# A decoder layer's out-projection as three single-pass products of halves, with all five engines' lists drawn up anew

## The chip, the cores and the metric

One core of one Trainium2 chip runs the whole kernel. The metric is the device time of one execution in microseconds (us). Five engines work side by side, each through its own list of instructions: TensorE (PE in the profile, its weight loads PEld), VectorE (DVE), ScalarE (ACT), GpSimd (POOL) and SyncE (SP, which here only issues transfers). They wait for each other by semaphores.

## The reference, cut to what matters

A post-norm decoder layer over 64 independent sequences (x is 64 x 256 x 256, the context 64 x 120 x 256). Only the first of its three parts is touched by the arithmetic of the change:

```python
zxbcdt = u @ W_in.T                      # u: 256 tokens x 256; z 512, xBC 544, dt 8 columns
xBC = silu(causal_conv4(xBC) + conv_b);  dt = softplus(dt + dt_bias)
y, _ = ssd(x * dt[..., None], A * dt, Bm, Cm, 64)      # 8 heads of 64
y = (y + x * D[:, None]).reshape(b, L, 512) * silu(z)
y = y * rsqrt(mean(y * y, axis=-1) + 1e-05) * norm_w
x = layernorm(x + y @ W_out.T)           # W_out: 256 x 512: the out-projection
x = layernorm(x + cross_attention(ctx, x))   # 8 heads, 120 + 256 keys
x = layernorm(x + twisted_ffn(x))            # three coupling cycles of a small net
```

## The kernel before

Every sequence is a set of steps (functions with the sequence's number as argument), and each engine has a written-out list of calls. After a fill for the first two sequences, a loop `for p in range(2, NSEQ - 1)` (61 passes) works on four sequences at a time: the last cycles of the feed-forward of f-2 and f-1, the attention of `f = p - 2`, the mixer of `a = p - 1`, and the first projections of `m = p`. After the loop a drain finishes the last ones. The order inside each engine's list is fixed text; nothing is reordered at run time, so an instruction whose semaphore is late holds all that stands behind it on its engine.

The steps that matter here, with their lines in the profile:

- PE: `project`/`product3` (L263) is a product of fp32 numbers as three passes of halves (hi x hi, lo x hi, hi x lo), used for w_in, wq, wkv and cw1. `y_pair(a, q)` (L338) multiplies the scan matrix Lm by xdt; `mean_square(a)` (L361) sums the squares; `out_proj(a)` (L350) is the out-projection in plain fp32: per sequence eight products of 128x128 by 128x256, which the profile records as sixteen matmuls. `scores(f, i, j)` (L443) are three products of halves of an attention score tile, `turn` (L455) transposes probabilities, `k_tile(a, 0)` (L263, kv_hi by wkv_hi) makes the first keys of sequence a, `layer(f-1, ., .)` (L518) is the feed-forward.
- DVE: `y_out(a, q)` (L1628) adds D*x to y straight from PSUM; `x_low` (L1487) and `kv_low(a, 1)` (L1719) subtract the high half from a value to get the low half; `x1_sum` (L1647), `x1_stats`, `x1_mean` (L1661), `x1_norm` (L1671) are the first layernorm, whose reciprocal root POOL makes (`mix`, L2504 to L2507); `pre(f-1, 0)` (L1852) updates the feed-forward's input; `weights(0, 3)` (L1903) scales w_out by norm_w at set-up.
- POOL: `gated(a, q)` (L2481) is g = yD * silu(z); `squares` (L2487, L2489) adds the squares that ACT made (`square`, L955).
- ACT: `x_high(m)` (L881) casts a 128x512 tile to the high half.

`out_proj(a)` waits for POOL's last `gated` (`l_g`), and comes right behind `mean_square(a)` in PE's list. `k_tile(a, 0)` waits for `kv_low(a, 1)`'s semaphore.

## Time and profile before

| | |
|---|---|
| median of 3 runs | 3686.18 us (3681.73 to 3687.39) |
| profiled execution, its own time | 3687.81 us |
| its span (first to last record) | 3685.6 us |
| mean granted TensorE clock | 0.991 |
| PE busy | 3613.6 us (98%) |
| DVE busy | 3246.4 us (88%) |
| ACT busy | 3072.9 us (83%) |
| POOL busy | 1788.0 us (49%) |

Busy times are unions of records, so an engine whose instructions follow each other with small gaps shows less than 100% though it never waits for anyone. 2.2 us of the execution's time lie outside its span. The execution profiled is 1.6 us above the median.

### The profile page before, as it was taken

How to read it: one execution, taken by the hardware profiler on the slowest of the kernel's cores; microseconds unless marked ns; L12 is line 12 of the kernel's file. 1: busy time of each engine (PE TensorE's matmuls, PEld its weight loads, DVE VectorE, ACT ScalarE, POOL GpSimd, SP SyncE). 2: the span in 40 equal slices, each digit the busy share in tenths (PEclk: the TensorE clock that was granted, in tenths of full speed). 3: DMA queues.
4: the chain of work that ended last, by engine and by line, in shares of the span. 5: the costliest groups of instructions: out<-in, count | busy, mean ns of one | idle time of the engine just before them, and what ended most of it. 6: DMA issues, size and time to landing. Idle time of an engine off the chain costs nothing.

```text
span 3685.6 us, 79670 instructions
## 1 busy us (share of the span) xinstructions
PE 3613.6 (98%) x26752; PEld 3085.0 (84%) x26752; DVE 3246.4 (88%) x7970; ACT 3072.9 (83%) x7559; POOL 1788.0 (49%) x3084
## 2 busy tenths in 40 slices
PE   5999999999999999999999999999999999999997
PEld 4888888888888888888888888888888888888885
DVE  7888988988988989889889889889898898898884
ACT  5788888888888888888888888888888888888884
POOL 4355454454554554554544545545545545445442
PEclk8999999999999999999999999999999999999998
DMA  3212212112122122122121121221221221211210
GB/s 100 59 37 67 59 42 67 52 49 67 39 63 64 37 67 64 37 67 58 43 67 53 48 67 39 63 65 37 67 64 37 67 60 42 67 55 46 67 34 21
DMA packets 312358, 203.28 MB, mean 55 GB/s; under 512 B 55056, under 2 KB 310928, under 8 KB 311952
## 3 DMA queue, kind: packets, MB, share of 16 engines
q1 hardware_dynamic: 311952, 198.20, 18.7%
q8 instruction: 215, 3.52, 0.4%
q14 instruction: 191, 1.56, 0.1%
HBM read 180.17 MB, written 17.96 MB: 54 GB/s over the span
## 4 chain that ended last, share of the span: by engine, by line
PE 93%; DVE 3%; ACT 1%; issue 1%; SPq 1%; DMA 1%; POOL 1%; POOLq 0%; DVEq 0%; ACTq 0%
PE psum L263 35%; PE psum L455 10%; PE psum L471 9%; PE psum L443 8%; PE psum L350 6%; PE psum L482 6%; PE psum L518 5%; PE psum L338 5%; PE psum L524 2%; PE psum L533 2%; PE psum L322 1%; PE psum L495 1%; PE psum L383 1%; PE psum L361 1%; PE psum L545 1%
## 5 line engine op out<-in xcount | busy, mean ns | idle before, releaser
L1015 ACT ACTIVATE prob<-psum,nmax 128x376 f32<-128x376 f32 x1024 | 588.7, 582 | 36.0 <-DVE nmax L1741 35.0
L2471 POOL TENSOR_TENSOR Lm<-Lm,G 128x384 f32<-128x384 f32 x512 | 497.3, 1011 | 81.8 <-DVE out_sb L1869 68.8
L1741 DVE TENSOR_REDUCE nmax<-psum 128x2 f32<-128x752 f32 x512 | 472.8, 934 | 44.2 <-PE psum L443 39.4
L455 PE MATMUL psum<-ident,prob 128*128 128x128 f32 (+1 forms) x3072 | 486.4, 278 | 3.1 <-DVE probT L1764 1.7
L455 PEld LDWEIGHTS psum<-ident,prob 128*128 128x128 f32 (+1 forms) x3072 | 354.8, 141 | 87.0 <-issue 46.5
L1493 DVE SCALAR_TENSOR_TENSOR u<-psum,par,u 128x255 f32<-128x255 f32 (+5 forms) x960 | 408.2, 467 | 12.0 <-ACT u L914 1.5
L2458 POOL TENSOR_SCALAR_AFFINE_SELECT Lm<-Lm 128x256 f32<-128x256 f32 x512 | 193.0, 416 | 375.7 <-DMA Lm<-cum_row 375.5
L2526 POOL TENSOR_TENSOR h_a<-h_a,cpl 128x512 f32<-128x512 f32 x64 | 83.0, 1297 | 594.0 <-DVE h_pre L1852 594.0
L471 PE MATMUL psum<-probT,V 128*64 128x256 f32 (+1 forms) x3072 | 360.5, 383 | 0.4 <-ACT probT L1025 0.4
L263 PE MATMUL psum<-x_hi,w_in_hi 128*128 128x256 f32 (+1 forms) x1152 | 344.8, 299 | 13.0 <-DVE w_in_lo L1897 7.6
L263 PE MATMUL psum<-x_hi,w_in_lo 128*128 128x256 f32 (+1 forms) x1152 | 325.4, 282 | 0.0
L263 PE MATMUL psum<-x_lo,w_in_hi 128*128 128x256 f32 (+1 forms) x1152 | 324.7, 282 | 0.0
L1025 ACT ACTIVATE probT<-psum 128x384 f32<-128x384 f32 x512 | 254.7, 498 | 79.6 <-PE psum L455 72.2
L1764 DVE COPY probT<-psum 128x384 f32<-128x384 f32 x512 | 281.4, 550 | 30.4 <-PE psum L455 30.2
L471 PEld LDWEIGHTS psum<-probT,V 128*64 128x64 f32 (+1 forms) x3072 | 208.6, 136 | 110.9 <-ACT probT L1025 0.4
L948 ACT ACTIVATE Lm<-Lm,ncum 128x256 f32<-128x256 f32 x512 | 264.8, 517 | 2.6 <-DVE ncum L1605 1.9
L263 PEld LDWEIGHTS psum<-x_hi,w_in_hi 128*128 128x128 f32 (+1 forms) x1152 | 214.0, 186 | 29.6 <-issue 21.2
L350 PE MATMUL psum<-w_out_sb,g 128*128 128x256 f32 x1024 | 236.8, 384 | 1.3 <-DVE dt_a L1507 1.3
L482 PE MATMUL psum<-wo_sb,oT 128*128 128x256 f32 x1024 | 235.5, 381 | 1.7 <-DVE probT L1764 1.4
L518 PE MATMUL psum<-h,cw_sb 128*128 128x256 f32 x768 | 209.3, 395 | 10.2 <-ACT h L1058 8.4
L1015 ACT ACTIVATION_READ_ACCUMULATOR prob<-psum,nmax 128x1 f32 x1024 | 218.7, 214 | 0.0
L2481 POOL TENSOR_TENSOR g<-xc,gate 128x256 f32<-128x256 f32 x256 | 206.5, 826 | 19.5 <-DVE xc L1628 19.4
(227 smaller groups left out, 11668.6 us busy)
## 6 DMA issues: line engine op xcount, KB each, us to landing
Lm<-cum_row SPq DMA_DIRECT2D x64, 1024.0 KB, 5.2
Lm<-cum_row SPq DMA_DIRECT2D x64, 512.0 KB, 6.6
invT<-inv_row SPq DMA_DIRECT2D x256, 128.0 KB, 3.0
xT_sb<-in_xT SPq DMA_DIRECT2D x64, 256.0 KB, 2.7
x_sb<-in_x SPq DMA_DIRECT2D x64, 256.0 KB, 5.8
result<-out_sb SPq DMA_DIRECT2D x64, 256.0 KB, 2.4
inv_row<-inv_t SPq DMA_DIRECT2D x512, 1.0 KB
ctx_sb<-in_ctx SPq DMA_DIRECT2D x64, 120.0 KB, 6.4
```

Source lines behind the costliest of these rows:

```text
L263: t = mm(dst, a, b, start=n == 1, stop=n == 3 * KT)
L350: t = mm(banks[b][:, i * D:(i + 1) * D], g[:, c, i * P:(i + 1) * P], w_out_sb[:, c, :], start=c == 0, stop=c == CT - 1)
L443: t = mm(banks[at[k]][:, 0:NK], q_[r, c, i * P:(i + 1) * P], k_[r, c, :], start=m == 0, stop=m == 2)
L455: t = tr(banks[b][0:m, j * P:(j + 1) * P], prob[:, r, j0:j0 + m], ident[:, :])
L471: t = mm(banks[b][k * HD:(k + 1) * HD, at:at + L], V[0:m, j, h * HD:(h + 1) * HD], probT[0:m, (8 * s + h) % HP, j, :], start=j == 0, stop= ...
L482: t = mm(banks[b][:, 0:D], oT[:, c, i * P:(i + 1) * P], wo_sb[:, c, :], start=c == 0, stop=c == CT - 1)
L518: t = mm(b[:, 0:L], cw2_sb[:, k, :], h1[:, k, :], start=k == 0, stop=k == KT - 1)
L1015: act(prob[:, r, :], b[:, 0:NK], ACT.Exp, bias=nmax[:, n:n + 1], accum_out=psum_row[:, n:n + 1]).then_inc(a_exp, 1)
L1493: stt(u[0:rows, c, d:L], src[:, 0:L - d], prm("conv_w", 4 * c + 3 - d, slice(0, rows)), u[0:rows, c, d:L], ALU.mult, ALU.add).then_inc(don ...
L1741: e.tensor_reduce(nmax[:, 2 * n:2 * n + 2], psum[:, b:b + 2, 0:NK], AX.X, ALU.max, negate=True).then_inc(d_max, 1)
L1764: cp(probT[:, (8 * s + 2 * c + k) % HP, :, i * P:(i + 1) * P], b[:, 0:len(JT) * P].rearrange("p (j t) -> p j t", j=len(JT))).then_inc(d_tn, 1)
L2471: t = tt(Lm[:, h, :], Lm[:, h, :], G[:, :], ALU.mult)
```

## The change

The out-projection is computed from halves: g is split into g_hi (ACT, `g_high`) and g_lo (DVE, `g_low`), w_out into w_out_hi and w_out_lo at set-up, and `project4` multiplies hi by hi, hi by lo and lo by hi, 24 products of 128x128 by 128x256 for a sequence. g_lo shares its memory with g, w_out_lo with w_out_sb. The scratch memory that the program keeps for dynamic DMA descriptors is set to 1024. And the lists of all five engines are written in a new order (some 1,500 of the 1,872 lines of the diff; the lines below show its core and one piece of the new order of PE and DVE).

```diff
-        w_out_sb, wo_sb = sb("w_out_sb", [P, CT, D]), sb("wo_sb", [P, CT, D])
+        w_out_hi, (w_out_lo, w_out_sb) = sb("w_out_hi", [P, CT, D], F32R), shared("w_out_lo", "w_out_sb", [P, CT, D])
-        g = sb("g", [P, CT, L])
+        g_hi, (g_lo, g) = sb("g_hi", [P, CT, L], F32R), shared("g_lo", "g", [P, CT, L])
...
+            def project4(dst, hi, lo, w_hi, w_lo, i):
+                tok = slice(i * P, (i + 1) * P)
+                for c in range(CT):
+                    mm(dst, hi[:, c, tok], w_hi[:, c, :], start=c == 0, stop=False)
+                    mm(dst, hi[:, c, tok], w_lo[:, c, :], start=False, stop=False)
+                    t = mm(dst, lo[:, c, tok], w_hi[:, c, :], start=False, stop=c == CT - 1)
+                return t
...
-                pe.wait_ge(l_g, 4 * s + 4)
+                pe.wait_ge(d_gl, 2 * s + 2)
                 for i in range(TT):
-                    for c in range(CT):
-                        t = mm(banks[b][:, i * D:(i + 1) * D], g[:, c, i * P:(i + 1) * P], w_out_sb[:, c, :],
-                               start=c == 0, stop=c == CT - 1)
+                    t = project4(banks[b][:, i * D:(i + 1) * D], g_hi, g_lo, w_out_hi, w_out_lo, i)
...
+            def g_high(s, j):
+                if not live(s):
+                    return
+                sc.wait_ge(l_g, 4 * s + 2 * j + 2)
+                act(g_hi[:, 2 * j:2 * j + 2, :], g[:, 2 * j:2 * j + 2, :], ACT.Copy).then_inc(a_gh, 1)
...
+            def g_low(s, j):
+                if not live(s):
+                    return
+                ve.wait_ge(a_gh, 2 * s + j + 1)
+                ve.wait_ge(a_sq, 4 * s + 2 * j + 2)
+                r = slice(2 * j, 2 * j + 2)
+                tt(g_lo[:, r, :], g[:, r, :], g_hi[:, r, :].bitcast(F32), ALU.subtract).then_inc(d_gl, 1)
...
-                    t.then_inc(set_w, 1)
+                    t.then_inc(set_split, 1)
+                    ve.wait_ge(set_split, 2)
+                    cp(w_out_hi[:, :, :], w_out_sb).then_inc(set_split, 1)
+                    ve.wait_ge(set_split, 3)
+                    tt(w_out_lo[:, :, :], w_out_sb, w_out_hi[:, :, :].bitcast(F32), ALU.subtract).then_inc(set_w, 1)
...
-    nc = bacc.Bacc("TRN2", target_bir_lowering=False, num_devices=1)
+    nc = bacc.Bacc("TRN2", target_bir_lowering=False, num_devices=1, dynamic_dma_scratch_size=1024)
```

PE, in the loop, where the scan's product stands among the attention's scores. Before, `y_pair(a, 0..3)` follows the last product of `q_pair(f, 1)`; it is these rows, and one score tile (`scores(f, 2, 0)`) stands behind it:

```order
L338 MATMUL psum<-Lm,xdt 64x256 x2
L338 MATMUL psum<-Lm,xdt 64x128 x2
L338 MATMUL psum<-Lm,xdt 64x256 x2
L338 MATMUL psum<-Lm,xdt 64x128 x2
L338 MATMUL psum<-Lm,xdt 64x256 x2
L338 MATMUL psum<-Lm,xdt 64x128 x2
L338 MATMUL psum<-Lm,xdt 64x256 x2
L338 MATMUL psum<-Lm,xdt 64x128 x2
L443 MATMUL psum<-k_hi,q_hi 128x376 x2
L443 MATMUL psum<-k_hi,q_lo 128x376 x2
L443 MATMUL psum<-k_lo,q_hi 128x376 x2
L263 MATMUL psum<-x_hi,w_in_hi 80x256
```

In the changed kernel (whose line numbers are 8 to 10 higher):

```order
L451 MATMUL psum<-k_lo,q_hi 128x376 x2
L348 MATMUL psum<-Lm,xdt 64x256 x2
L348 MATMUL psum<-Lm,xdt 64x128 x2
L348 MATMUL psum<-Lm,xdt 64x256 x2
L348 MATMUL psum<-Lm,xdt 64x128 x2
L348 MATMUL psum<-Lm,xdt 64x256 x2
L348 MATMUL psum<-Lm,xdt 64x128 x2
L348 MATMUL psum<-Lm,xdt 64x256 x2
L348 MATMUL psum<-Lm,xdt 64x128 x2
L451 MATMUL psum<-k_hi,q_hi 128x376 x2
L451 MATMUL psum<-k_hi,q_lo 128x376 x2
L451 MATMUL psum<-k_lo,q_hi 128x376 x2
```

One score tile moved ahead of the scan's product, and another one that stood next to a third tile later in the list now stands alone behind it.

DVE, in the loop, from the first `y_out(a, 0)`. Before, between the `y_out`s and the convolution's taps (L1493):

```order
L1628 SCALAR_TENSOR_TENSOR xc<-xc,par,psum 128x256
L1493 SCALAR_TENSOR_TENSOR u<-psum,par,u 80x255
L1507 TENSOR_SCALAR dt_a<-psum,par 8x256
L1493 SCALAR_TENSOR_TENSOR u<-psum,par,u 80x254
L1479 TENSOR_SCALAR x<-x,mv_att,rs_att 128x256
L1733 TENSOR_TENSOR k_lo<-psum,k_hi 128x376
```

In the changed kernel, where `g_low(a, 0)` is L1803 (the second one, `g_low(a, 1)`, comes behind the taps, ahead of `softplus(m)` and `mean_square(a)`):

```order
L1515 SCALAR_TENSOR_TENSOR u<-psum,par,u 80x255
L1529 TENSOR_SCALAR dt_a<-psum,par 8x256
L1515 SCALAR_TENSOR_TENSOR u<-psum,par,u 80x254
L1803 TENSOR_TENSOR g_lo<-g,g_hi 128x512
L1515 SCALAR_TENSOR_TENSOR u<-psum,par,u 80x253
L1515 SCALAR_TENSOR_TENSOR u<-psum,par,u 128x255
```

A 128x512 subtraction entered the stretch that begins with the `y_out`s. At the end of that stretch stands `kv_low(a, 1)`. Before:

```order
L1608 COPY dt_tok<-dc 32x16 x4
L1712 CAST kv_hi<-kv 128x2x256
L1755 STREAM_TRANSPOSE inv_t<-row_inv 128x32
L1719 TENSOR_TENSOR kv_lo<-kv,kv_hi 128x2x256
L1852 TENSOR_TENSOR h_pre<-h_pre,h_a 128x512
```

In the changed kernel:

```order
L1741 TENSOR_TENSOR kv_lo<-kv,kv_hi 128x2x120
L1871 TENSOR_TENSOR h_pre<-h_b,cpl 128x512
L1734 CAST kv_hi<-kv 128x2x256
L1882 TENSOR_TENSOR h_pre<-h_pre,h_a 128x512
L1741 TENSOR_TENSOR kv_lo<-kv,kv_hi 128x2x256
```

`pre(f-1, 0)` (h_pre<-h_pre,h_a) stood behind `kv_low(a, 1)` and stands ahead of it now. Between the first `y_out(a, 0)` and `kv_low(a, 1)` in all, one `top` (a maximum over scores, L1741 before), `bc_silu` (two instructions, L1523 and L1524 before), `x1_keep(a, 0)` (L1680 before), `out_x(f-2, 0)` (L1860 before) left the stretch; two `g_low`, `x_silu(m, 0)` (128x512), `pre(f-1, 0)`, one `out_norm` and one `out_stats` (128x256 each) entered it. In the changed kernel `x1_norm(a, 0)` comes 6 steps behind `x1_mean(a, 1)`, with `kv_high(a, 0)`, `turn_out(f, 6)`, `inverse(f, 0)`, `out_mean(f-2, 0)` and `turn_dc(m)` between.

## Rows read from the trace of the kernel before

**Rows 1.** The page: span, busy time (share of the span), instructions of each engine

```profile
span 3685.6 us, 79670 instructions
PE 3613.6 (98%) x26752; PEld 3085.0 (84%) x26752; DVE 3246.4 (88%) x7970; ACT 3072.9 (83%) x7559; POOL 1788.0 (49%) x3084
```

**Rows 2.** Busy time by stretch: length, engines, granted clock, DMA share, GB/s

```profile
1000.00:2000.00 1000.00, 999.31 (x7470) 854.70 (x7470) 898.54 (x2209) 853.63 (x2107) 498.69 (x859) 1.00 0.19 56
```

**Rows 3.** Timeline of PE around the out-projection: start us, length us, instruction

```profile
1720.14 3.70 PE L350 MATMUL psum<-w_out_sb,g 128*128 128x256 f32 x16
1723.49 0.47 PE L263 MATMUL psum<-x2T_hi,cw_hi 128*128 128x256 f32 x1
1723.79 0.28 PE L263 MATMUL psum<-x2T_hi,cw_lo 128*128 128x256 f32 x1
1723.91 0.28 PE L263 MATMUL psum<-x2T_lo,cw_hi 128*128 128x256 f32 x1
```

**Rows 4.** Timeline of PE from one scan product to the next

```profile
1708.75 2.87 PE L338 MATMUL psum<-Lm,xdt 128*64 128x256 f32 x32
...
1737.98 0.44 PE L263 MATMUL psum<-kv_hi,wkv_hi 128*128 128x376 f32 x1
...
1738.95 0.33 PE L263 MATMUL psum<-kv_lo,wkv_hi 128*128 128x376 f32 x1
1739.30 1.10 PE L518 MATMUL psum<-h,cw_sb 128*128 128x256 f32 x4
...
1764.75 2.82 PE L338 MATMUL psum<-Lm,xdt 128*64 128x256 f32 x32
1767.50 0.44 PE L443 MATMUL psum<-k_hi,q_hi 64*128 64x376 f32 x2
...
1768.20 0.35 PE L263 MATMUL psum<-x_hi,w_in_hi 128*80 128x256 f32 x1
```

**Rows 5.** Timeline of DVE in that pass, with idle before and releaser

```profile
1710.36 0.45 DVE L1628 SCALAR_TENSOR_TENSOR xc<-xc,par,psum 128x256 f32<-128x256 f32 x1
1710.73 0.69 DVE L1487 TENSOR_TENSOR x_lo<-xT_sb,x_hi 128x512 fp32r<-128x512 f32 x1
...
1726.58 0.18 DVE L1661 BATCH_NORM_AGGREGATE mv_mix<-st_mix 128x2 f32<-128x6 f32 x1
...
1729.73 0.41 DVE L1671 TENSOR_SCALAR x_n<-x,mv_mix,rs_mix 128x256 f32<-128x256 f32 x1
...
1733.47 0.41 DVE L1830 TENSOR_SCALAR cpl<-cpl,tf_gain,c_cyc 128x256 f32<-128x256 f32 x1 [0.28 <-ACT cpl L1070]
...
1736.93 0.68 DVE L1719 TENSOR_TENSOR kv_lo<-kv,kv_hi 128x512 fp32r<-128x512 f32 x1
1737.53 0.68 DVE L1852 TENSOR_TENSOR h_pre<-h_pre,h_a 128x512 f32<-128x512 f32 x1
```

**Rows 6.** Timeline of POOL in that pass

```profile
1710.89 2.50 POOL L2481 TENSOR_TENSOR g<-xc,gate 128x256 f32<-128x256 f32 x3 [0.20 <-DVE xc L1628]
...
1714.33 0.75 POOL L2481 TENSOR_TENSOR g<-xc,gate 128x256 f32<-128x256 f32 x1
...
1717.07 1.28 POOL L2487 TENSOR_TENSOR gate<-gate 128x512 f32<-128x512 f32 x1 [0.72 <-ACT gate L955]
...
1727.93 1.03 POOL L2507 TENSOR_TENSOR rs_mix<-ve_mix,minus_half 128x4 f32<-128x4 f32 x1
```

**Rows 7.** ACT in 1000 to 2000 us, groups: count, busy us, mean ns

```profile
L881 ACT ACTIVATE x_hi<-xT_sb 128x512 fp32r<-128x512 f32 x18 | 11.2, 623 | 0.0
```

**Rows 8.** All 64 of DVE's x_low: duration ns, min/median/max

```profile
L1487 DVE TENSOR_TENSOR x_lo<-xT_sb,x_hi x64: 681/684/694, 4.7 to 3500.8; 128x512 fp32r<-128x512 f32 x64
```

**Rows 9.** Timeline of DVE at the start

```profile
13.15 2.03 DVE L1493 SCALAR_TENSOR_TENSOR u<-psum,par,u 128x255 f32<-128x255 f32 x5 [1.09 <-ACT u L914]
18.50 2.84 DVE L1903 TENSOR_SCALAR w_out_sb<-w_out_sb,par 128x256 f32<-128x256 f32 x4 [3.31 <-DMA gw_sb<-in_gw]
```

More of the change, by code:

```diff
@@ L812, in _ @@
             scores(last, 2, 0)
+            turn(last, 3)
+            k_tile(last, 3)
+            scores(last, 2, 1)
+            x2_turn(last - 1)
             v_tile(last, 1)
[L814 to L817 removed]
             turn(last, 4)
@@ L2141, in _ @@
-                k_low(a, 2)
-            last = NSEQ - 1
-            x_dt(last - 1, 1)
+            last = NSEQ - 1
+            top(last - 3, 7)
+            turn_out(last - 3, 10)
+            gain(last - 4, 0)
+            turn_inverse(last - 3, 0)
+            kv_low(last - 2, 0)
+            twisted_part(last - 4, 0)
+            kv_high(last - 2, 1)
+            kv_low(last - 2, 1)
+            pre(last - 4, 0)
+            conv_tap(last - 1, 3, 0)
+            conv_tap(last - 1, 2, 0)
+            inverse(last - 3, 1)
@@ new lines, in _ @@
+            conv_tap(last - 1, 2, 1)
+            context_stats(last - 1)
+            conv_tap(last - 1, 3, 1)
+            conv_tap(last - 1, 3, 2)
+            conv_tap(last - 1, 2, 2)
+            k_low(last - 2, 0)
+            by_token(last - 1)
+            x_silu(last - 1, 1)
+            turn_inverse(last - 3, 1)
+            q_low(last - 2, 0)
+            k_low(last - 2, 1)
+            gain(last - 4, 1)
+            twisted_part(last - 4, 1)
+            x_dt(last - 1, 0)
+            pre(last - 4, 1)
@@ L2149, in _ @@
             bc_low(last - 1)
-            divide(last - 3, 1)
-            top(last - 2, 1)
             out_x(last - 4, 1)
+            turn_out(last - 2, 0)
             out_tw(last - 4, 1, 0)
             out_tw(last - 4, 1, 1)
+            x2_raw(last - 3, 0)
+            x2_stats(last - 3, 0)
+            out_stats(last - 4, 1)
+            out_mean(last - 4, 1)
+            x2_mean(last - 3, 0)
+            out_x(last - 4, 0)
             top(last - 2, 2)
-            turn_out(last - 2, 0)
@@ L2157, in _ @@
-            x2_raw(last - 3, 0)
             gate_silu(last - 1, 1)
-            context_stats(last - 1)
-            out_stats(last - 4, 1)
-            x_low(last)
             q_low(last - 2, 1)
-            out_mean(last - 4, 1)
+            x1_keep(last - 2, 0)
             x2_raw(last - 3, 1)
             x2_stats(last - 3, 1)
+            x2_mean(last - 3, 1)
             top(last - 2, 3)
-            x2_stats(last - 3, 0)
-            context_mean(last - 1)
-            x2_mean(last - 3, 1)
+            top(last - 2, 4)
@@ L2208, in _ @@
-            cum_da(last)
-            x1_mean(last - 1, 1)
-            kv_high(last - 1, 0)
-            turn_out(last - 2, 8)
+            conv_tap(last, 1, 1)
+            conv_tap(last, 0, 1)
+            conv_tap(last, 1, 2)
+            conv_tap(last, 0, 2)
+            g_low(last - 1, 1)
+            x2_high(last - 3)
+            softplus(last)
+            x1_keep(last - 2, 1)
+            mean_square(last - 1)
+            x2_low(last - 3)
+            context_n(last - 1)
+            turn_out(last - 2, 4)
@@ L2212, in _ @@
+            x1_sum(last - 1, 0)
+            x1_sum(last - 1, 1)
+            cum_dt(last)
+            x1_stats(last - 1, 0)
+            x_silu(last, 0)
+            cum_da(last)
+            inverse(last - 2, 0)
+            x1_stats(last - 1, 1)
+            x1_mean(last - 1, 0)
+            cum_scan(last)
+            x1_mean(last - 1, 1)
+            out_norm(last - 4, 1)
+            turn_out(last - 2, 6)
+            turn_inverse(last - 2, 0)
+            top(last - 2, 6)
             x1_norm(last - 1, 0)
-            x1_norm(last - 1, 1)
@@ L2322, in _ @@
             pre(last - 2, 0)
+            k_low(last, 0)
+            divide(last - 1, 0)
             inverse(last - 1, 1)
-            k_low(last, 0)
-            turn_inverse(last - 1, 1)
+            out_stats(last - 3, 0)
+            out_mean(last - 3, 0)
             q_low(last, 0)
+            x1_keep(last, 1)
+            out_norm(last - 3, 0)
             k_low(last, 1)
@@ L2388, in _ @@
             divide(last, 1)
-            out_stats(last - 2, 1)
-            out_mean(last - 2, 1)
             x2_raw(last, 0)
             x2_stats(last, 0)
+            out_x(last - 1, 1)
             x2_mean(last, 0)
-            out_mean(last - 2, 0)
             x2_raw(last, 1)
@@ L2419, in _ @@
             pre(last, 1)
-            out_stats(last - 1, 0)
-            out_mean(last - 1, 0)
-            out_norm(last - 1, 0)
             out_x(last, 1)
@@ L2579, in _ @@
             po.wait_ge(set_dve, 1)
-            weights(0)
+            context(0)
             masked(0, 0)
@@ L2592, in _ @@
             gated(0, 3)
-            context(0)
             squares(0)
+            weights(0)
             inv_rms(0)
```

951 lines of the change are left out of this document (467 added, 484 removed).

## The prediction

> **What bounds the kernel now.** I read the page first: PE is busy 98% of the span, no other engine above 88% [rows 1]. A share over the whole span can hide stages, so the second view is the busy time by stretch: between 1000 and 2000 us PE is busy 999.31 of 1000.00 us at a granted clock of 1.00, DVE 898.54 and ACT 853.63 [rows 2]. The loop is PE's work end to end, and a microsecond taken from PE's list counts as long as nobody else becomes late. Third, the timeline gives the length of a pass: the scan product L338 starts at 1708.75 and again at 1764.75, so a pass takes 56.00 us, and 61 passes are 3416 of the 3685.6 us [rows 1, 4].
>
> The important question is how much room the other engines have, and for DVE the 90% misleads: instructions follow each other there at start-to-start distances below their lengths (L1719 lasts 0.68 and the next starts after 0.60 [rows 5]), and small instructions leave gaps in which nobody is waited for. So I measure a stretch from PE's event that releases DVE to DVE's event that releases PE. `y_out(a, 0)` waits for PE's second scan pair and starts at 1710.36, 1.61 us behind 1708.75 (in the five passes that follow it is 1.61 or 1.62 too). Behind it DVE works down its list to `kv_low(a, 1)`, which ends at 1736.93 + 0.68 = 1737.61, 27.25 us later [rows 5]. `k_tile(a, 0)` needs that and starts at 1737.98 [rows 4]: DVE has 0.37 us of room there. That is less than what the change moves on either engine, and the forecast hangs on it.
>
> **The change part by part, for one pass.**
>
> *The product.* L350 starts at 1720.14; the product behind it starts at 1723.49, and the one behind that at 1723.79: 3.65 us [rows 3]. Single-pass products of 256 columns follow each other at 0.12 (1723.79 to 1723.91 [rows 3]). 24 of them, an entry of 0.08 as the first of such a run has over the others, and one 0.12 to the same point make 24 x 0.12 + 0.08 + 0.12 = 3.08: **-0.57** on PE. By the Trainium skill, page "TensorE: Matmul & The Clock Gate", section "Back-to-back issue gap", products at full clock are N/2.4 + 2.5 ns apart, 109 ns for 256 columns. By that the 24 would take 0.2 us less than by the row, some 13 us in all; the row is of this kernel, with its weight loads, and I keep the row.
>
> *PE's new order.* One score tile, `scores(f, 2, 0)`, moves from the part behind L338 to the part ahead of it. Inside a run three pairs of 376 columns cost 3 x 0.17 = 0.51 (five such products take 1738.95 - 1737.98 = 0.97, the first of them 0.28 [rows 4]). A tile that stands alone costs 1768.20 - 1767.50 = 0.70 [rows 4]; the new list has one more that stands alone, `scores(f, 1, 0)`: 0.19, and 0.07 on the product ahead of it. `layer(f-1, 1, 1)` starts 1739.30 - 1738.95 = 0.35 behind the product ahead of it where 0.17 is the distance [rows 4]; that is a short wait for `h`, which comes from `pre(f-1, 0)`. Since `pre` stands ahead of `kv_low(a, 1)` now, I take 0.19 off. PE's own pass is then 56.00 - 0.57 + 0.26 - 0.19 - 0.05 (one joint fewer between kinds of product) = 55.45.
>
> From L338 to `k_tile(a, 0)` it was 1737.98 - 1708.75 = 29.23 [rows 4] and becomes 29.23 - 0.57 - 0.51 - 0.05 = 28.10. From there to the next L338 it was 26.77 and becomes 26.77 + 0.51 + 0.26 - 0.19 = 27.35.
>
> *DVE's stretch.* Out of it go `top` 0.85, `bc_silu` 0.86, `x1_keep` 0.32, `out_x` 0.25 and an `out_mean` 0.09: 2.37. Into it come two `g_low`, which are the shape and operation of `kv_low(a, 1)`, whose successor starts 1737.53 - 1736.93 = 0.60 behind [rows 5]: 1.20; `x_silu(m, 0)`, 128x512 too, 0.60; `pre(f-1, 0)`, which stood behind `kv_low(a, 1)` and stands ahead of it, 0.60; `out_norm` 0.30, `out_stats` 0.29, `out_mean` 0.09: 3.08. Net **+0.71**. (The small ones are their usual start-to-start distances; a quarter of their sum wrong would be 0.1.)
>
> *The layernorm's round trip.* Behind `x1_mean(a, 1)` at 1726.58 POOL makes the reciprocal root, done at 1727.93 + 1.03 = 1728.96 [rows 6]; `x1_norm(a, 0)` came at 1729.73 [rows 5] and did not wait. What stands between the two now adds up to 1.95, while the trip takes 1728.96 - 1726.58 = 2.38: a new wait of 0.35 to 0.5. I take **+0.35**.
>
> *What the stretch has to give.* In its 27.25 us DVE has pauses; the one with a releaser is 0.28 at L1830 [rows 5], all of them (distance less the kind's usual one) are 1.2. If every pause but the new one went, the stretch would be 27.25 - 1.21 + 0.71 + 0.35 = 27.1; if every one stayed, 27.25 + 0.71 = 27.96, and with the new one 28.3. The pauses behind `y_out` come from the hand-overs with PE and ACT, and these keep their order, but the others are short waits that shift. I take the nearer middle, **27.5**.
>
> *The sum of a pass.* 1.61 + 27.5 + 0.07 (as far as a semaphore takes) + 27.35 = 56.5, against 55.45 that PE would need. By the ends of the stretch it is 56.1 and 57.0. PE's list gets shorter by 0.55 and waits 1.1, in part at `out_proj(a)` already, whose `g_low(a, 1)` stands behind six taps and comes about half a microsecond late, in part at `k_tile(a, 0)`. Those two waits are one delay, not two: what PE loses at the first it doesn't lose again at the second. 0.52 x 61 = **+31.7**.
>
> *ACT.* Two casts of 128x512 per sequence at 0.62 [rows 7] are 1.25 on an engine busy 853.63 of 1000.00 us [rows 2]: 87%. They stand in the part where squares and scores are made, and are followed by exponentials that PE's transposes wait for; I cost them at nothing more, since PE is waiting for DVE by then; without that cover each would be 0.62.
>
> *Set-up.* `weights(0, 3)` on DVE starts at 18.50 behind a transfer, 2.84 long [rows 9]. It gains a subtraction of 128x1024, twice the 0.60 of 128x512, and a cast of that size, which I take at 0.9 (one input less): 2.1. The five convolution taps that ran at 13.15 (2.03 us), ahead of that transfer's end, now come behind it [rows 9]. Some of the 4.1 is hidden by POOL and the context's transfer now stands ahead of the weights': **+5**. The drain's list is redrawn too; its bound is +-4 by the same kind of moves. 
>
> 3687.8 + 31.7 + 5 = 3724.5 for an execution like the profiled one, which was 1.6 above the median of the runs: **3723**.
>
> **The rivals.**
>
> *A: the waits hide and PE stays the bound (other side).* DVE's stretch has to be 28.10 - 1.68 = 26.4 or less; its list as it was, less all pauses, is 26.0, and 0.71 comes on top. So it needs `out_norm`, `out_stats` and the round trip to cost nothing, or DVE to be released earlier than 1.61 behind L338. PE is then left with 55.45 a pass: 3687.8 - 0.55 x 61 + 5 - 1.6 = 3658. Chance 0.13.
>
> *B: the lower end of the stretch.* 27.1, a pass of 56.1: 3687.8 + 0.1 x 61 + 5 - 1.6, some 3697; with less at the start 3692. For it speaks that a list whose engine is late runs without its pauses. Against it, that the pauses behind `y_out` are hand-overs. Chance 0.22, a third of it within 0.2% of before.
>
> *C: `g_low` and POOL block each other.* Three L2481, the first beside the 128x512 subtraction `x_low` at 1710.73, take 2.50, the fourth alone 0.75 [rows 5, 6]: POOL loses about 2.50 - 3 x 0.75 = 0.25 next to a subtraction with two operands. `g_low(a, 0)` lands beside L2487 (1.28 long [rows 6]), whose end `mean_square(a)` waits for. If that, or DVE itself, is held for such an instruction's length once per pass, a pass is 57.3 to 57.8: 3765 and more. Against DVE being held: 64 `x_low` beside `gated` last 681 to 694 ns, none longer [rows 8]. The Trainium skill, page "SBUF — State Buffer", section "SBUF: two separate sides", says that a DVE instruction with two inputs from SBUF and a GpSimd instruction that reads SBUF exclude each other and the later one waits for the whole of the first. `g_low` is such an instruction. The trace agrees as far as POOL's loss goes; it has no case in which DVE came second. Chance 0.08.
>
> **How the numbers follow.** The main case (stretch of 27.3 to 27.9) has 0.50 and gives 3705 to 3748; B 0.22; A 0.13; C 0.08; 0.07 is for something smaller than A between PE's bound and before. The range for 8 in 10 leaves out A and C: 3684 to 3756. What a measurement tells from no change is about 0.2%, 3679 to 3694: faster 0.17, same 0.10, slower 0.73.
>
> **What would show it.** In the changed trace: L350's 3.65 us replaced by about 3.0; PE idle in the loop, some 1.1 us a pass, before `out_proj` (released by DVE's L1803) and before the first kv_hi by wkv_hi product (released by L1741); PE's busy share in 1000 to 2000 us down to 98%; the pass 56.5; DVE idle before `x1_norm` on POOL's L2507 line. The prediction is wrong if DVE's stretch from `y_out(a, 0)` to the end of `kv_low(a, 1)` is 26.4 or less, or if PE waits anywhere else by more than it does there.

## The result, and the profile after

| | before | changed |
|---|---|---|
| median (runs) | 3686.61 us (4; 3681.73 to 3687.39) | 3747.14 us (4; 3745.76 to 3752.71) |
| ratio, 95% interval | 1 | 1.0170 [1.0152, 1.0187] |
| profiled execution / its span | 3687.81 / 3685.6 us | 3745.76 / 3744.0 us |

The change makes the kernel 60.5 us slower. The forecast was 3723 (3684 to 3756), some 36 us slower: the sign holds, the time lies inside the range, at the upper edge of the main case (3705 to 3748), and the wait that was forecast is the one that is there. The size was 36 us where 60 came.

The page of the changed kernel, the same lines as [rows 1], and its busy times by stretch as in [rows 2]:

```profile
span 3744.0 us, 81023 instructions
PE 3599.0 (96%) x27264; PEld 3083.0 (82%) x27264; DVE 3350.7 (89%) x8100; ACT 3125.7 (83%) x7686; POOL 1803.6 (48%) x3084
```

```profile
1000.00:2000.00 1000.00, 979.76 (x7480) 842.52 (x7478) 915.99 (x2223) 856.83 (x2108) 492.06 (x835) 1.00 0.19 54
```

PE is busy 14.6 us less in the whole and is no longer busy without a break: 979.76 of 1000 where it was 999.31. The view of waits says for whom it waits, PE alone, 1000 to 2000 us (us in total, times, longest):

```profile
PE psum L265 <- DVE kv_lo L1741: 12.7, 18, 0.9
PE psum L451 <- DVE k_lo L1755: 2.2, 6, 0.4
PE psum L463 <- DVE x L1813: 2.2, 4, 0.7
```

18 passes, 18 waits for `kv_low(a, 1)`: this is the wait that was forecast. The timeline of PE in one pass shows it and the product, as in [rows 3, 4]:

```profile
996.95 0.44 PE L348 MATMUL psum<-Lm,xdt 128*64 128x256 f32 x2
...
1007.72 0.58 PE L369 MATMUL psum<-ones,gate 128*128 128x2 f32 x4
1008.36 0.36 PE L277 MATMUL psum<-w_out_hi,g_hi 128*128 128x256 f32 x1
...
1011.26 0.28 PE L265 MATMUL psum<-x2T_hi,cw_hi 128*128 128x256 f32 x1
1011.38 0.28 PE L265 MATMUL psum<-x2T_hi,cw_lo 128*128 128x256 f32 x1
...
1026.28 0.41 PE L265 MATMUL psum<-kv_hi,wkv_hi 128*128 128x376 f32 x1 [0.65 <-DVE kv_lo L1741]
...
1053.55 0.65 PE L348 MATMUL psum<-Lm,xdt 128*64 128x256 f32 x4
```

From the first product of `project4` to the second one behind it: 11.38 - 8.36 = 3.02 us where L350 had 3.65. This pass is 1053.55 - 996.95 = 56.60 long, and PE stands 0.65 us before the first key product. DVE's stretch in the same pass, as in [rows 5]:

```profile
998.52 0.48 DVE L1650 SCALAR_TENSOR_TENSOR xc<-xc,par,psum 128x256 f32<-128x256 f32 x1
...
1025.44 0.69 DVE L1741 TENSOR_TENSOR kv_lo<-kv,kv_hi 128x512 fp32r<-128x512 f32 x1
```

It is 1025.44 + 0.69 - 998.52 = 27.61 us, and 1.57 + 27.61 + 0.15 + 27.27 is the pass. The table has the same measures over 56 passes in the middle of each trace. They are my own sums over the records; "short" is the mark that a tenth of the passes are under, and the last column is the time between the 3rd and the 63rd scan product.

| us per pass | scan product to first key product, short / mean | key product to next scan product, short / mean | pass, short / mean | DVE's stretch, mean | 60 passes |
|---|---|---|---|---|---|
| before | 29.19 / 29.22 | 26.76 / 26.87 | 55.97 / 56.09 | 27.24 | 3364.7 |
| changed | 29.31 / 29.45 | 27.25 / 27.50 | 56.57 / 56.96 | 27.74 | 3415.8 |

So of the 58.4 us by which the span grew, 51.1 lie in the 60 passes. Of these, 0.60 x 60 = 36 us are in every pass, and 0.27 x 60 = 16 us come from uneven passes: 30 of the 56 are 0.3 to 2.5 us longer than the short ones, where before 7 were, by at most 0.9. The start has 5.8 more (first scan product at 46.37 for 45.09; from there to the second 46.37 for 41.85), the end 1.4.

### The profile page after: what moved, and what is told of

It is laid out like the page before. It is cut to its first block, busy times and chain, and to the rows that moved or that the text cites. A ratio compares the mean times of both kernels' runs of the same rounds, so it can differ in the third digit from the quotient of the medians.

```text
span 3744.0 us, 81023 instructions
## 1 busy us (share of the span) xinstructions
PE 3599.0 (96%) x27264; PEld 3083.0 (82%) x27264; DVE 3350.7 (89%) x8100; ACT 3125.7 (83%) x7686; POOL 1803.6 (48%) x3084
## 4 chain that ended last, share of the span: by engine, by line
PE 41%; DVE 39%; issue 8%; POOL 6%; DMA 3%; ACT 2%; SPq 1%; DVEq 0%; POOLq 0%; ACTq 0%
PE psum L265 17%; PE psum L490 5%; DVE u L1515 5%; DVE nmax L1763 5%; PE psum L463 4%; PE psum L479 4%; PE psum L526 3%; PE psum L451 3%; DVE xc L1650 2%; POOL rs_mix L2561 2%; DVE probT L1786 2%; DVE kv_lo L1741 2%; PE psum L532 2%; DVE x L1501 2%; DVE x L1669 1%
## 5 line engine op out<-in xcount | busy, mean ns | idle before, releaser
L1763 DVE TENSOR_REDUCE nmax<-psum 128x2 f32<-128x752 f32 x512 | 470.8, 929 | 2.7 <-PE psum L451 2.5
L2512 POOL TENSOR_SCALAR_AFFINE_SELECT Lm<-Lm 128x256 f32<-128x256 f32 x512 | 207.1, 438 | 549.3 <-DMA Lm<-cum_row 549.3
L1515 DVE SCALAR_TENSOR_TENSOR u<-psum,par,u 128x255 f32<-128x255 f32 (+5 forms) x960 | 404.4, 470 | 3.2 <-ACT u L897 0.9
L2580 POOL TENSOR_TENSOR h_a<-h_a,cpl 128x512 f32<-128x512 f32 x64 | 105.3, 1645 | 402.6 <-DVE h_pre L1882 402.6
L490 PE MATMUL psum<-wo_sb,oT 128*128 128x256 f32 x1024 | 245.4, 383 | 1.7 <-DVE oT L1795 1.5
L265 PE MATMUL psum<-kv_hi,wkv_hi 128*128 128x376 f32 x512 | 187.6, 366 | 43.3 <-DVE kv_lo L1741 43.0
L451 PE MATMUL psum<-k_hi,q_hi 64*128 64x376 f32 x1024 | 212.6, 411 | 15.3 <-DVE k_lo L1755 8.6
L265 PEld LDWEIGHTS psum<-x_hi,w_in_lo 128*128 128x128 f32 (+1 forms) x1152 | 214.8, 186 | 0.2
```

The costliest lines, as they stand in the source:

```text
L265: t = mm(dst, a, b, start=n == 1, stop=n == 3 * KT)
L451: t = mm(banks[at[k]][:, 0:NK], q_[r, c, i * P:(i + 1) * P], k_[r, c, :], start=m == 0, stop=m == 2)
L490: t = mm(banks[b][:, 0:D], oT[:, c, i * P:(i + 1) * P], wo_sb[:, c, :], start=c == 0, stop=c == CT - 1)
L1515: stt(u[0:rows, c, d:L], src[:, 0:L - d], prm("conv_w", 4 * c + 3 - d, slice(0, rows)), u[0:rows, c, d:L], ALU.mult, ALU.add).then_inc(don ...
L1763: e.tensor_reduce(nmax[:, 2 * n:2 * n + 2], psum[:, b:b + 2, 0:NK], AX.X, ALU.max, negate=True).then_inc(d_max, 1)
```

## The experiments

Theory 1: VectorE's stretch from `y_out(a, 0)` to `kv_low(a, 1)` sets the pass. Theory 2: the new lists cost what was lost, on other engines. Ratios are to the kernel before on the same chip; the changed kernel has 1.0170. "The stretch" is VectorE's, and a pass is given short or mean as in the table.

**e2: VectorE's stretch shortened by 0.6, by a step that others wait for.** VectorE's list has the end of the stretch at the head of the next pass, whose f - 2 and f are this pass's f - 1 and a.

```diff
-                pre(f - 2, 0)
                 kv_low(f, 1)
+                pre(f - 2, 0)
```

> The changed kernel with one swap in VectorE's loop: the subtraction kv_low of the layernormed tile goes ahead of the feed-forward's addition pre, which it stood behind. Theory 1 (the pass is set by VectorE's stretch from the first y_out to the end of that kv_low, 27.60 us in the changed kernel): the stretch loses the 0.60 us of pre, the wait of TensorE before the first key product shrinks by as much, and if 0 to 0.4 us of it comes back as a later feed-forward input, a pass is 56.0 to 56.4 instead of 56.57 and the time is 12 to 37 us below the changed kernel's 3747, so 3710 to 3735. Theory 2 (the loss lies in the new order of the other engines and in transfers that come late, and VectorE's stretch only happens to end late): no change beyond 5 us, 3742 to 3752.

1.0178 [1.0163, 1.0193]: no gain, which is theory 2's number. The stretch did fall (mean 27.30, short 27.13) and the first key product came 0.46 earlier (28.85), but the part behind it grew from 27.25 to 27.86. `pre(f-1, 0)` feeds `layer(f-1, 1, 1)`, two steps behind in PE's list, so the wait only moved. The swap that I had read as "into the stretch, 0.60" had given PE 0.6 elsewhere.

**e7: the same 0.6, by a step that nobody waits for soon.**

```diff
                 context_stats(a)     # head of the next pass: a is m of the last one
+                x_silu(a, 0)
                 x_silu(a, 1)
...
                 x2_high(f - 1)
-                x_silu(m, 0)
                 x2_low(f - 1)
```

The fill and the drain have the same move.

> The changed kernel with x_silu(m, 0), a 128x512 instruction of 0.60 us on VectorE, taken out of the stretch from y_out to kv_low and put back where it stood before, behind k_low(a, 0), beside its twin. Theory 1 (VectorE's work in that stretch sets the pass; unlike the addition that e2 moved, nothing between waits for this one): the stretch falls from 27.60 to 27.0, a pass from 56.57 to 56.0, the time by 30 to 37 us: a ratio of 1.007 to 1.009. Rival (VectorE is full all around the pass, and what leaves one stretch makes the next one late): TensorE waits as much behind the scan product's next start; no change beyond 5 us, ratio 1.0155 to 1.0185.

1.0106 [1.0088, 1.0124]: 24 us less, where 30 to 37 were expected. The stretch is 27.12 (short), the first key product comes at 28.83, the part behind it stays at 27.25, the pass is 56.09. The waits of PE, 1000 to 2000 us, kernel e7:

```profile
PE psum L265 <- DVE kv_lo L1741: 3.9, 18, 0.5
PE psum L463 <- DVE x L1813: 3.2, 5, 0.7
PE psum L451 <- DVE k_lo L1755: 2.5, 8, 0.4
```

12.7 us became 3.9. Theory 1 stands: 0.48 us less of VectorE's stretch are 0.48 us less of the pass. That it is 0.48 for an instruction of 0.60 says that 0.12 came back as pauses in the stretch. In the mean the pass gains only 0.40 (56.56), because its uneven passes got longer: VectorE waits 41.9 us for the spread inverse sums of the softmax in e7, and 33.9 in the changed kernel.

**e4: the new lists with the old arithmetic.** The edit is the diff of the change taken back in `out_proj` and `weights`, and all calls of `g_high` and `g_low` left out; the lists stay as new.

> The changed kernel's lists on all engines with the old arithmetic: out-projection in plain fp32, g_high and g_low left out, w_out not split. Theory 1: VectorE's stretch loses 1.2 us and ends in time; TensorE is the bound again with its old product, a pass of 56.0 to 56.2, and with the longer fill (some 5 us) the time is 3690 to 3705. Theory 2 (the new order itself costs what was lost): a pass stays at 56.5 and more, 3725 to 3750.

1.0119 [1.0102, 1.0136]: the time is theory 2's. The pass is 56.34 short, a little under its 56.5, and 56.74 mean. PE's part behind the key product is 27.26, half a microsecond above before, since a score tile moved there. In the part ahead of it the product is 0.6 dearer again. VectorE has 1.2 us less of work, but its stretch is only 0.25 shorter (27.35), and PE still starts the key product 0.15 behind `kv_low`, so it still waits there. By my sums over the records VectorE waits 0.5 us a pass in that stretch, nearly all of it for ScalarE, where the changed kernel has next to none of over 0.1 us. The new order alone costs 42 us, some 22 of them in every pass (0.37 x 60).

**e3: the old lists with the new arithmetic.**

```diff
                 square(a, 1)
+                g_high(a, 0)
...
                 square(a, 3)
+                g_high(a, 1)
...
                 x2_norm(f - 1, 0)
+                g_low(a, 0)
...
                 conv_tap(m, 0, 2)
+                g_low(a, 1)
                 top(f, 5)
```

> The kernel before with its own lists and only the new arithmetic: the out-projection as 24 single-pass products, g_high put behind the second and the fourth square on ScalarE, g_low behind the second layernorm of the attention and behind the six taps on VectorE, w_out split at set-up. Theory 1: VectorE's stretch grows from 27.2 by 1.2 to 28.4, or by what its pauses do not take up; with 1.6 ahead and 26.8 behind a pass is 56.5 to 57.0, so 3715 to 3750: the arithmetic alone is slower than before by 30 to 60 us. Theory 2 (it is the new order that costs): the product's 0.57 us show as a gain or vanish, 3650 to 3695.

1.0229 [1.0214, 1.0244], 83 us above before, more than the 30 to 60 expected; 72 of them lie in the 60 passes, the rest in the start and the end. The pass is 57.11 short and DVE's stretch 28.34: of the 1.2 us that were put in, 1.14 show. But PE does not stand at the key product. The waits of PE in this kernel, 1000 to 2000 us, and one of ScalarE's:

```profile
PE psum L526 <- ACT h_a L1094: 8.7, 17, 0.5
PE psum L503 <- DVE x L1501: 4.7, 18, 0.3
```

```profile
ACT prob L1023 <- DVE nmax L1763: 29.0, 18, 1.6
```

VectorE's lateness reaches PE earlier in the pass, by two ways: by `x2_norm` (L503), and by ScalarE. The maximum over the scores (`top(f, 5)`, L1763) stands behind `g_low(a, 1)`; ScalarE's exponential waits 1.6 us for it where before it waited 0.5, and its list has no pause from there to the feed-forward's gelu, whose result L526 takes. The key product behind them then finds its operand. The stretch is the right measure of the delay, but the place where PE waits is the first one whose operand is late.

**e11: only PE's product, in the old lists.** w_out is split at set-up, g is not: all 24 products take one tile filled at set-up. The run leaves out the projection of g, with ScalarE's casts and VectorE's subtractions.

```diff
-                    t = project4(banks[b][:, i * D:(i + 1) * D], g_hi, g_lo, w_out_hi, w_out_lo, i)
+                    t = project4(banks[b][:, i * D:(i + 1) * D], g_hi, g_hi, w_out_hi, w_out_lo, i)
```

> The kernel before with its own lists, and of the change only TensorE's part: w_out is split at set-up and out_proj is 24 single-pass products, but g is not split: all 24 take one tile that was filled once at set-up, and out_proj still waits for the last gated product. So the projection's values are not the reference's; the time is that of the products without ScalarE's casts and VectorE's subtractions. Theory 1 (VectorE's stretch leaves TensorE 0.37 us in the kernel before, and the product gives 0.57): 0.37 to 0.45 us less a pass, 55.6 to 55.65, and 4 us more of set-up: 17 to 23 us less than before, a ratio of 0.994 to 0.9955. Rival (the product's whole gain shows, since VectorE's stretch moves up with it): 0.57 a pass and a ratio of 0.9915 to 0.993.

0.9951 [0.9935, 0.9968]: 18 us less, the number of theory 1, but not for its reason. PE's timeline in e11:

```profile
1044.04 0.36 PE L277 MATMUL psum<-w_out_hi,g_hi 128*128 128x256 f32 x1
...
1046.95 0.28 PE L265 MATMUL psum<-x2T_hi,cw_hi 128*128 128x256 f32 x1
1047.07 0.28 PE L265 MATMUL psum<-x2T_hi,cw_lo 128*128 128x256 f32 x1
...
1049.75 0.37 PE L380 MATMUL psum<-ident,ctx_sb 120*128 120x120 f32 x2
1050.26 1.10 PE L526 MATMUL psum<-h,cw_sb 128*128 128x256 f32 x4
```

ScalarE's gelu that makes `h`, before the change and then in e11:

```profile
1725.28 0.84 ACT L1058 ACTIVATE h<-psum,par 128x256 f32<-128x256 f32 x2 [0.40 <-PE psum L263]
```

```profile
1047.49 1.28 ACT L1072 ACT_TABLE_LOAD   x1
1048.79 0.84 ACT L1072 ACTIVATE h<-psum,par 128x256 f32<-128x256 f32 x2
```

1047.07 - 1044.04 = 3.03, so 0.62 are gained there, and the pass is 0.37 (short) shorter. Three microseconds later L526 starts 0.51 behind L380 where before had 0.27 (1726.48 to 1726.75): PE reaches `layer(f-1, 0, 1)` 0.6 earlier, and its input `h` comes from ScalarE's gelu. Before, the gelu waited 0.40 for PE; now it starts at once behind ScalarE's own table load and is the later one. The 0.24 are lost there. PE waits nowhere for `kv_low` in this run. VectorE's stretch shrank along to 26.86 (mean), mostly by one pause: the 0.28 for `cpl` [rows 5], which ScalarE makes from PE's product, is gone.

The distance from the end of `kv_low(a, 1)` to the key product is 0.36 to 0.37 before, in e3 and in e11, with stretches of 27.24, 28.38 and 26.86 (means). In the old lists the two engines moved together, so the 0.37 that the prediction called room was no reserve that a longer stretch could use up. In the new lists it is 0.15 in every kernel here.

e3, e4 and e11 have the new scratch size too. e11 is faster than before all the same, which leaves no visible price for it.

**e1 and e6: the passes that are longer than the others.** In the changed kernel VectorE waits 33.9 us, 36 times, for the spread inverse sums of the softmax (before: 5.1 us, 11 times), which the transfer queue sends out to memory and spreads back over the partitions. DVE and the transfer queue in a long pass (PE's scan product starts it at 1053.55):

```profile
1090.60 0.20 DVE L1777 STREAM_TRANSPOSE inv_t<-row_inv 128x32 f32<-128x32 f32 x1
...
1101.36 0.69 DVE L1795 TENSOR_TENSOR oT<-oT,invT 128x512 f32<-128x512 f32 x1 [1.53 <-DMA invT<-inv_row]
```

```profile
1089.59 0.54 SPq L2795 DMA_DIRECT2D c_row<-cpl  x2
1094.82 0.38 SPq L2803 DMA_DIRECT2D c_col<-c_row  x1
1095.30 1.31 SPq L2776 DMA_DIRECT2D inv_row<-inv_t  x4
1096.66 0.40 SPq L2752 DMA_DIRECT2D x_sb<-in_x  x1
1097.52 1.24 SPq L2786 DMA_DIRECT2D invT<-inv_row  x2
```

I first took the 256 KB load of x between the two legs for the cause.

```diff
                 keep_inv(f, 1)
-                load_x(m)
                 spread_inv(f, 1)
                 spread_c(f - 1, 1)
+                load_x(m)
```

> The changed kernel with one step of the transfer queue moved: load_x(m), 256 KB, goes from between the two halves of the round trip of the softmax sums (keep_inv, spread_inv of the second half) to behind both spreads. Theory: the passes that are 0.3 to 2 us longer than the others between the first key product and the next scan product are those in which the spread sums arrive late behind this load; with the load out of the way they go back to what they were before, which is 8 us less over the loop: 3735 to 3742. Rival: the late arrivals come from the queue's own unevenness or from VectorE issuing the sums late: no change, 3744 to 3750.

1.0178 [1.0162, 1.0193], no gain: the rival's number. The rows say what is late instead: the sums are ready at 1090.60 + 0.20 = 1090.80 and issued at 1095.30. SyncE stands in `spread_c(f-1, 0)` (L2803), which waits for L2795's transfer to land, and `keep_inv(f, 1)` (L2776) is behind it in its list.

```diff
-                spread_c(f - 1, 0)
                 keep_inv(f, 1)
+                spread_c(f - 1, 0)
```

> The changed kernel with one swap in the transfer queue's loop: keep_inv(f, 1), which sends the second half of the softmax's inverse sums, goes ahead of spread_c(f-1, 0). In the changed kernel VectorE has the sums ready at 36.9 us behind the scan product, but SyncE issues them at 40.2, since it waits in spread_c for the round trip of keep_c; before, they were issued at 36.9. Theory: the transfer then has 3 us of room again, the wait for the spread sums (33.9 us in all, 36 times) falls to what it was before (5.1 us, 11 times), and the time falls by 8 to 15 us: a ratio of 1.0130 to 1.0148. Rival: the late passes come from elsewhere (the coefficients' own transfer, c_col, is as late), no change beyond 3 us.

1.0131 [1.0116, 1.0146]: 14 us less, as expected. The pass is 56.57 short as before the edit and 56.70 in the mean where it was 56.96. The queue in e6, and the waits for the sums, changed kernel first, then e6:

```profile
1029.12 0.53 SPq L2795 DMA_DIRECT2D c_row<-cpl  x2
1030.36 1.28 SPq L2776 DMA_DIRECT2D inv_row<-inv_t  x4
1033.12 0.38 SPq L2803 DMA_DIRECT2D c_col<-c_row  x1
```

```profile
  DMA invT<-inv_row: 33.9, 36
```

```profile
  DMA invT<-inv_row: 6.2, 6
```

**e5: two engines in each other's way.** What is left of the uneven passes in the changed kernel: in 17 of 56 the way from the scan product to `mean_square` is 0.40 longer. DVE and POOL in a short pass (scan product at 1168.29), then in a long one (at 1111.32), changed kernel:

```profile
1170.26 0.69 DVE L1509 TENSOR_TENSOR x_lo<-xT_sb,x_hi 128x512 fp32r<-128x512 f32 x1
...
1172.04 0.50 DVE L1501 TENSOR_SCALAR x<-x,mv_att,rs_att 128x256 f32<-128x256 f32 x1
...
1170.25 0.78 POOL L2501 TENSOR_SCALAR ve_att<-mv_att 128x1 f32<-128x1 f32 x1
1171.11 0.57 POOL L2503 TENSOR_TENSOR rs_att<-ve_att,minus_half 128x1 f32<-128x1 f32 x1
1171.65 2.86 POOL L2535 TENSOR_TENSOR g<-xc,gate 128x256 f32<-128x256 f32 x4
```

```profile
1113.29 0.68 DVE L1509 TENSOR_TENSOR x_lo<-xT_sb,x_hi 128x512 fp32r<-128x512 f32 x1
...
1115.06 0.89 DVE L1501 TENSOR_SCALAR x<-x,mv_att,rs_att 128x256 f32<-128x256 f32 x1
...
1113.24 0.22 POOL L2501 TENSOR_SCALAR ve_att<-mv_att 128x1 f32<-128x1 f32 x1
1113.54 0.86 POOL L2503 TENSOR_TENSOR rs_att<-ve_att,minus_half 128x1 f32<-128x1 f32 x1
1114.38 2.87 POOL L2535 TENSOR_TENSOR g<-xc,gate 128x256 f32<-128x256 f32 x4
```

A POOL instruction of one column takes 0.22 or 0.78, by whether it begins 0.05 us ahead of `x_low` (1113.24 and 1113.29) or together with it (1170.25 and 1170.26). If it slips in ahead, POOL's gated products stand 0.3 us earlier against VectorE's list, and `x2_norm` (L1501) then lasts 0.89 instead of 0.50. The two cases do not mix: in all 17 long passes L2503 starts 2.22 to 2.26 us behind the scan product, in the 39 others 2.82.

The records also show what the 0.89 is made of (my sums, an estimate). Less the 0.40 that L1501 takes undisturbed, it ends 0.48 us behind the start of the gated product beside which it began, in all 56 passes (0.475 to 0.490). In the short pass it begins 0.39 into a product (1172.04 to 1171.65) and loses 0.1; in the long one it begins together with the second product (at 1115.07, by the single records) and loses all 0.48. A product's record is 0.73 long.

```diff
                 y_out(a, 3)
-                x2_norm(f - 1, 0)
                 top(f, 5)
...
                 bcdt_tap(m, 1)
+                x2_norm(f - 1, 0)
                 g_low(a, 0)
```

> The changed kernel with one VectorE step moved: x2_norm(f-1, 0), a 128x256 instruction on one SBUF tile with two pointer operands, goes from behind the last y_out, where GpSimd's gated products run, to ahead of g_low(a, 0). In the changed kernel it lasts 0.42 to 0.50 us in two passes of three and 0.89 in the third, and those passes are 0.40 longer from one scan product to mean_square. Theory (the two engines exclude each other there, as the Trainium skill, page SBUF - State Buffer, section SBUF: two separate sides, has it): the 0.4 us go in a third of the passes, 8 us in all; ratio to before 1.0150 where the changed kernel has 1.017. Rival (the odd passes come from a late operand): the same 0.4 appears at another place, no change within 3 us.

1.0194 [1.0179, 1.0209]: slower, where 1.0150 was expected. The long passes are gone (short and mean are both 11.06 to `mean_square`, where the changed kernel has 10.76 and 10.89), and every pass is 0.30 longer instead. DVE in e5:

```profile
1004.84 0.48 DVE L1515 SCALAR_TENSOR_TENSOR u<-psum,par,u 80x255 f32<-80x255 f32 x1 [0.26 <-ACT u L897]
```

`x2_norm` had filled the time until ACT delivers the tap's input. The collision needs `x2_norm` at that place: GpSimd's early pattern still comes in e5, and no pass is long by it. But it cost 0.12 a pass in the mean, and its cure 0.30.

**e8, e10, e9: together.** e8 has the moves of e5, e6 and e7; e10 those of e6 and e7; e9 is e10 with `g_low(a, 0)` of the loop on GpSimd:

```diff
                 att(f - 1, 1)
+                g_low(a, 0)          # GpSimd; taken out of VectorE's list
                 squares(a)
```

> The three moves of e5, e6 and e7 together in the changed kernel. If each is a cause of its own, the gains add up: 8 + 11 + 33 us less than the changed kernel's 1.017, a ratio of 1.000 to 1.006, that is, level with the kernel before or up to 20 us slower, the rest being the longer fill. If VectorE is full all around the pass, or if the late transfers only hide behind the other waits, 1.010 or more.

> The changed kernel with the moves of e6 (softmax sums first in the transfer queue) and e7 (x_silu out of VectorE's stretch), without that of e5. The two gave 1.0131 and 1.0106 alone where the changed kernel has 1.017. If they are separate causes: 1.0065 to 1.0080. If the late transfers only showed because VectorE was late, less than that adds up: 1.009 or more.

> e10's kernel with g_low(a, 0) in the loop made by GpSimd, between att(f-1, 1) and squares(a), instead of VectorE; g_low(a, 1) stays on VectorE. Theory 1: VectorE's stretch loses another 0.60 us (27.1 to 26.5), and TensorE's own work is next to a bound: a pass of 55.6 to 55.9, of which some 0.3 is mean_square coming later since GpSimd has 1.28 us more ahead of it and only 0.7 of them were idle. Time 25 to 40 us below e10, a ratio of 0.996 to 1.001: level with the kernel before. Rival: GpSimd's longer chain to mean_square takes back all that VectorE gives, because out_proj then starts as late: a pass as in e10, ratio 1.006 or more.

e8 1.0085 [1.0068, 1.0102], e10 1.0048 [1.0033, 1.0063], e9 1.0061 [1.0046, 1.0076]. e10's two moves gave 14 and 24 us alone and 45 together, more than either expectation had. The surplus fits the waits for the spread sums, which e7 alone had made longer: in e10 they are 5.6 us, 5 times. e8 lies between its two expectations: e5's move takes back a part (its short pass is 56.39, e10's 56.11). In e9 the rival's number comes, but not by its mechanism: `mean_square` starts 10.71 or 10.98 behind the scan product, little later than in e10 (10.77). VectorE's stretch is 27.07 short and 27.30 mean, for e10's 27.13 and 27.25, though 0.60 of work left it. VectorE reaches the taps before their input, and right behind, the collision comes again:

```profile
995.80 0.48 DVE L1515 SCALAR_TENSOR_TENSOR u<-psum,par,u 128x255 f32<-128x255 f32 x1 [0.18 <-ACT u L922]
996.20 0.81 DVE L1501 TENSOR_SCALAR x<-x,mv_att,rs_att 128x256 f32<-128x256 f32 x1
```

In 44 of 56 passes VectorE waits these 0.18 and the second L1501 of the pass takes 0.79 to 0.87 beside POOL's `g_low`, where 0.40 is usual; in the 12 others the first L1501 takes 0.88 beside a gated product. So the collision, which 14 passes of e10 have, is in every pass of e9, and it takes 0.4 of the 0.6.

**e12: the start.**

```diff
             context(0)
+            weights(0)               # GpSimd, was between squares(0) and inv_rms(0)
             masked(0, 0)
```

> e10's kernel (both moves) with GpSimd's weights(0), the split of the feed-forward's first weights, put back from between squares(0) and inv_rms(0) to ahead of its first scan work, where it stood in the kernel before and where GpSimd waits for a transfer anyway. In the changed kernel it keeps the first sequence's reciprocal root waiting (60.22 us where before had 57.72), and the stretch from the first to the second scan product is 46.4 us where before had 41.9. Theory: 3.0 to 3.8 us of those 4.5 go, the stretch is 43.3 to 44.0 in place of e10's 47.1, and the ratio is 1.0037 to 1.0042 where e10 has 1.0048. Rival (VectorE's own longer set-up, the split of w_out and the taps behind it, is what is late, and the root only waits along): less than 1 us, 46 to 47.

1.0059 [1.0045, 1.0073]; from the first scan product to the second 48.4 us, e10 has 47.1. The theory falls (it expected 43.3 to 44.0), and the rival's 46 to 47 is not met either. PE still waits for VectorE's sixth tap ahead of `out_proj(0)` (in the changed kernel [1.40 <-DVE u L1515], before 1.28), and the root is not what `x1_sum` waits for. How much the move itself is worth cannot be read from this run, since in 40 to 60 us PE's granted clock (the third number from the end) differed. Changed kernel, then e12:

```profile
40.00:60.00 20.00, 12.26 (x83) 10.06 (x84) 13.81 (x30) 13.06 (x32) 17.69 (x21) 0.85 0.05 14
```

```profile
40.00:60.00 20.00, 15.20 (x82) 12.23 (x81) 12.16 (x26) 11.29 (x29) 15.00 (x21) 0.61 0.07 21
```

More of e12's 20 us lie at the lower of the two levels (1.2 GHz) than of the changed kernel's. e1, e2, e5 and e6 have the changed kernel's start unaltered and reach the second scan product 0.1 to 2.3 us later than it, so differences of that size say nothing. What the new start costs, 4 to 12 us to the second scan product over the kernels here (e4 4.4, changed 5.8, e10 7.6, e12 12.2), stays open.

## Why the prediction was right, and where its size was off

- *The product*: 3.08 forecast, 3.02 measured. Right. 24 products take 2.80 to 2.91 to the next one, 0.117 to 0.121 each. By the Trainium skill, page "TensorE: Matmul & The Clock Gate", section "Back-to-back issue gap", 109 ns for 256 columns is the gap of an isolated product, and the section says itself that it is off for a stream with weight loads; the sum by it would be 2.8, an estimate. The row decides.
- *PE's order*: 27.35 forecast from the key product to the next scan product, 27.25 measured. Right, and e4 shows the half microsecond with the old arithmetic too.
- *DVE's stretch*: 27.5 forecast, 27.61 measured. Right in sum, and that is luck: two errors cancel. The layernorm's round trip was to cost a wait of 0.35; it costs none, since POOL made its three instructions in 1.62 us where they had been 2.10 (ending 1.89 behind the start of the second mean, where [rows 5, 6] gave 2.38), and `x1_norm` follows VectorE's step ahead of it without a pause. And of the 1.2 us of pauses only some 0.35 went, by the sum 27.25 + 0.71 - 27.61, where I had assumed 0.8.
- *The hand-over*: 0.07 was put for the semaphore, which no row showed. From the end of `kv_low` to the key product it is 0.15 in every pass; from PE to the first `y_out` it is 1.57 where 1.61 was put.
- *The pass*: 56.5 forecast, 56.57 in the short ones. Of the 1.1 us of PE's waits, half a microsecond was named for `out_proj`, which leaves 0.6 for the key product. Measured are 0.65 at the key product and 0.27 at `out_proj`: L277 starts 1008.36 - 1007.72 = 0.64 behind L369, and before L350 (1720.14 [rows 3]) was 0.37 behind this row:

```profile
1719.77 0.51 PE L361 MATMUL psum<-ones,gate 128*128 128x2 f32 x4
```

  In the changed kernel `g_low(a, 1)` ends 0.14 ahead of L277 (DVE L1803, 1007.54 + 0.68), so that is the operand that came last. The view of waits does not list this one; the gap that it sees before L277 is under 0.1 us. The rest is small waits at L451 for `k_lo`, 0.2 a pass.
- *The step that was mis-sized* is the loop's term, "0.52 x 61 = +31.7". It took every pass for the short one. 16 us more came from uneven passes, by two causes that were put at nothing. The first is SyncE's new order, which moved `keep_inv(f, 1)` behind a step that waits for a transfer's round trip: taking that back (e6) gives 14 us. I had costed the order of PE and VectorE, and of the transfer queue only the start. The second is the collision at `x2_norm`, 0.12 a pass, 7 us. The two make more than 16 because the kernel before had uneven passes as well, 0.12 x 60 = 7 us, and e6 removes nearly all unevenness behind the key product (0.02 a pass is left, where before had 0.11).
- *Set-up* +5: 5.8 came. e12 gives no sign that POOL's `weights(0)` is the cause, and the part of w_out's split is not shown: e4, without it, still has 4.4, and starts with the same list differ by up to 2.3 us.
- *ACT's casts*, put at nothing: no run takes them out alone. PE's waits between 1000 and 2000 us name no instruction of ACT, which agrees. ACT was not free in general, though: in e3 and e11 it is ACT's list that makes L526 late.
- *Rival C* was half right: VectorE can be held by GpSimd. The trace of before had this too, where the prediction says that it has no case: two of its 128 L1479 (`x<-x,mv_att,rs_att`) take 0.79 and 0.82, in the drain, beside POOL's products. By the Trainium skill, page "SBUF — State Buffer", section "SBUF: two separate sides", whichever of the two starts first keeps the port and the other waits for the whole instruction. I had weighed it on `g_low`, whose 128x512 stayed at 0.67 to 0.71 in all but one of 128 (0.92, in the drain); it struck L1501, 128x256 with one tensor as input. The page names two-input instructions and those in a two-port mode; which mode L1501 has no run here shows. The records agree with a lock that the first one keeps, but L1501 goes on 0.48 us behind the start of a product whose record is 0.73 long, so by these records it does not wait for the whole (a profile's spans on GpSimd are rough). That `g_low` holds POOL up is seen as well: the second L2503 of a pass takes 1.08 to 1.10 instead of 0.56 in 41 of 62 passes, and `g_low` begins within 0.02 of it (1003.43 and 1003.45).

What the parts are worth, by kernels: the product alone is -18 us, the casts and subtractions in the old lists +101 (e3 less e11), the new lists with the old arithmetic +42, and the new arithmetic in the new lists some 18 on top of these (1.0170 less 1.0119). So the lists are better fitted to the new arithmetic than the old ones, and are worse than the old ones without it. The best kernel with the new arithmetic found here (e10) is still 0.5% slower than before.
